# The opening of layer 0: banks and signals of their own for the first two batches, VectorE normalising them, and three small loads moved to SyncE

## What is computed

```
x = x + L0_xattn(layernorm(x), ctx, ctx)      # 16 heads of 8 features, softmax, biases bq, bk, bv, bo
x = x + L0_ffn(layernorm(x))                  # 8 experts, chosen per position by affinity to waff
x = x + L1_xattn(layernorm(x), ctx)           # 16 heads of 64 features, its own layernorms, one null key
x = x + L1_ffn(layernorm(x))                  # gate, up and down with rounded weights and activations

def L0_xattn(q, k, v):                        # per batch
    q, k, v = q @ Wq.T + bq, k @ Wk.T + bk, v @ Wv.T + bv
    attn = softmax(q_h @ k_h.T / sqrt(8))     # per head h
    return concat(attn @ v_h) @ Wo.T + bo
```

## Time and profile before

| | us |
|---|---|
| median of three runs | 879.06 |
| lowest and highest | 878.26 and 881.53 |
| the profiled execution, its own time | 880.04 |
| its span in the profile | 878.3 |
| PE busy | 810.5 (92%) |
| DVE busy | 698.3 (80%) |
| POOL busy | 482.5 (55%) |
| ACT busy | 443.5 (50%) |

### The profile page before, as it was taken

How to read it: one execution, slowest core, us unless ns; L and a number is a source line. 1 busy time by engine, 2 the same in 40 slices (tenths; PEclk the granted TensorE clock), 3 DMA queues, 4 the chain that set the end, 5 groups by cost and what they waited for, 6 DMA issues and landing times. The chain is left out here.

```text
span 878.3 us, 29798 instructions
## 1 busy us (share of the span) xinstructions
PE 810.5 (92%) x11109; PEld 674.8 (77%) x11139; DVE 698.3 (80%) x1919; ACT 443.5 (50%) x1077; POOL 482.5 (55%) x975
## 2 busy tenths in 40 slices
PE   4999999997499997899999999999999999999983
PEld 2777777775498886778888888888888888888861
DVE  3889989875514555478999999899999999999876
ACT  2666666654055564344555545455455554555442
POOL 7567678875512224244655656466564655656243
PEclk9999999998789997799999999999999999999995
DMA  9766330000655662021211212112121121211110
GB/s 242 273 247 247 119 104 14 15 20 26 166 149 142 162 159 69 10 60 35 56 45 35 69 36 60 45 36 69 35 64 41 47 57 35 66 39 48 42 32 12
DMA packets 57666, 70.91 MB, mean 81 GB/s; under 512 B 8002, under 2 KB 34482, under 8 KB 57522
## 3 DMA queue, kind: packets, MB, share of 16 engines
q1 hardware_dynamic: 42226, 44.55, 19.9%
q10 hardware_dynamic: 13248, 20.26, 6.3%
q0 software_dynamic: 2048, 4.20, 1.6%
HBM read 44.61 MB, written 24.37 MB: 79 GB/s over the span
## 5 line engine op out<-in xcount | busy, mean ns | idle before, releaser
L1943 ACT ACTIVATE a_pT<-psum 128x512 f32<-128x512 f32 x128 | 69.5, 595 | 40.8 <-PE psum L1745 22.2
L664 DVE TENSOR_REDUCE l_mx<-psum 128x4 bf16<-128x512 f32 x128 | 81.8, 680 | 7.4 <-remote 4.4
L2107 DVE TENSOR_REDUCE a_mxf<-psum 128x4 f32<-128x512 f32 x128 | 81.0, 673 | 3.1 <-PE psum L1718 3.1
L1473 POOL TENSOR_TENSOR f_hd<-f_hmc,f_wmean 128x1 f32<-128x1 f32 x32 | 6.7, 211 | 135.0 <-DVE f_hr L2224 134.2
L1650 PEld LDWEIGHTS psum<-a_cTm,a_Wk 128*128 128x128 f32 x512 | 67.8, 199 | 15.7 <-issue 14.4
L499 ACT ACTIVATE l_pT<-psum 128x512 f32<-128x512 f32 x128 | 71.2, 598 | 14.4 <-PE psum L385 13.8
L1638 PEld LDWEIGHTS psum<-a_xT,a_Wq 128*128 128x128 f32 x512 | 66.1, 196 | 15.3 <-issue 14.4
L1700 PE MATMUL psum<-a_Wv,a_cTm 128*128 128x512 f32 x128 | 73.7, 658 | 0.8 <-DVE a_kT L2095 0.6
L1726 PE MATMUL psum<-a_qT,a_kT 64*128 64x128 f32 x1024 | 71.8, 281 | 0.0
L1638 PE MATMUL psum<-a_xT,a_Wq 128*128 128x128 f32 x512 | 71.1, 283 | 0.5 <-ACT a_xT L1926 0.5
L1467 POOL TENSOR_SCALAR f_hq<-f_ht 128x512 bf16<-128x512 f32 x31 | 60.3, 1945 | 20.0 <-ACT f_ht L1988 19.9
(11 more groups left out here) (308 smaller groups left out, 2244.3 us busy)
## 6 DMA issues: line engine op xcount, KB each, us to landing
sorted_x<-r_zeros ACTq DMA_DIRECT2D x12, 1408.0 KB, 5.9
a_r_all<-a_r_rows SPq DMA_DIRECT2D x62, 256.0 KB
e_w<-in_E_W1b SPq DMA_DIRECT2D x39, 258.0 KB, 2.8
e_xt<-sorted_x SPq DMA_DIRECT2D x39, 64.0 KB, 2.4
sorted_y<-e_yt ACTq DMA_DIRECT2D x39, 64.0 KB, 2.7
a_cin<-in_ctx SPq DMA_DIRECT2D x32, 64.0 KB
out<-f_x SPq DMA_DIRECT2D x32, 64.0 KB
x_res<-in_x SPq DMA_DIRECT2D x1, 512.0 KB, 7.2
```

The lines of the kernel that those rows point to most:

```text
L664: nc.vector.tensor_reduce(mx[:, s, Q4 * k:Q4 * k + Q4], maxp[k % 2].rearrange("p (h t) -> p h t", h=Q4), AX_X, ALU.max).then_inc(mx_ready, 1)
L1943: nc.scalar.activation(pT[:, 2 * half + e, :], tp[e], ACT.Exp, scale=SCALE).then_inc(exp_ready, 1)
L2107: nc.vector.tensor_reduce(mxf[:, hh:hh + 4], maxp[e].rearrange("p (h t) -> p h t", h=Q4), AX_X, ALU.max).then_inc(mxf_ready, 1)
```

## The change

Five edits, all in `attention_routing_block`.

1. **Banks and signals.** For the batches 0 and 1, k, q and v go to six different banks: k to `tp[0]` and `tp[2]`, q to `tp[1]` and `tp[3]`, v to `yp` and `xp`; the transposed x of batch 1 goes to `tp[2]`. Each of the six matmuls signals for itself, and each copy waits for its own alone. `q_spread` of these batches no longer waits for `k_copy`, and `x_transpose(1)` no longer for `v_copy(0)`. New waits: `max_scores(0, 0)` for k and q of batch 0, `scores(0)` for k and q of batch 1, `expert_sums` for `v_copy(0)`.
2. **Normalisation.** POOL makes only `l_rs` for the two batches, and DVE makes `l_xn` (a `tensor_scalar` of its own). POOL waits until both are made before its second memset of ones. `x_norm(2)` on POOL moves ahead of the small constants.
3. **Signals of the loads.** bv leaves `w_in`, of which now five loads are awaited; it counts on `v_in` together with both memsets of ones, and only `v_copy` of 0 and 1 wait for that.
4. **Loads.** waffT, bo and wo are issued by SP, after its eighth load (batches 4 to 7), no longer by ACT.
5. **Order.** PE does `x_transpose(1)`, `max_scores(0, 0)` and then `projections(1)`. DVE goes: statistics and normalisation of 0, the same of 1, `q_spread(0)`, `v_copy(0)`, `x_stats(2)`, two `maxima`, `q_spread(1)`, two `maxima`, `v_copy(1)`, `x_stats(3)`.

```diff
@@ -122,7 +122,7 @@
-    ones_set = sem("l0_ones_set")
+    v_in = sem("l0_v_in")
@@ -141,7 +141,14 @@
-    N_W, N_O = 6 * 16, 3 * 16
+    first_k, first_q, first_v = (tp[0], tp[2]), (tp[1], tp[3]), (yp, xp)
+    N_W, N_O, N_V = 5 * 16, 3 * 16, 16 + 2
...
+    def projected(b, part):
+        return 3 * b + part if b < 2 else b + 5
...
+    def first_x(b):
+        return tp[2][:, 0:S] if b == 1 else xp[:, 0:S]
@@ -157,6 +164,8 @@
+            if i == 3:
+                late_loads(sp)
@@ -165,10 +174,12 @@
-        act.dma_start(bv_row[:], w["bv"].partition_broadcast(P)).then_inc(w_in, 16)
-        act.dma_start(rt["waffT"][:], wr["waffT"]).then_inc(rsem["w_in"], 16)
-        act.dma_start(bo_row[:], w["bo"].partition_broadcast(P)).then_inc(rsem["w_in"], 16)
-        act.dma_start(wo[:], w["Wo"]).then_inc(rsem["w_in"], 16)
+        act.dma_start(bv_row[:], w["bv"].partition_broadcast(P)).then_inc(v_in, 16)
...
+    def late_loads(sp):
+        sp.dma_start(rt["waffT"][:], wr["waffT"]).then_inc(rsem["w_in"], 16)
+        sp.dma_start(bo_row[:], w["bo"].partition_broadcast(P)).then_inc(rsem["w_in"], 16)
+        sp.dma_start(wo[:], w["Wo"]).then_inc(rsem["w_in"], 16)
@@ -183,12 +194,15 @@
     def pool_part(g, after_setup, before_loop):
...
-        def x_norm(b, s):
+        def x_rsqrt(b, s):
...
+        def x_norm(b, s):
+            x_rsqrt(b, s)
@@ -257,14 +271,15 @@
-        x_norm(0, 0)
-        nc.gpsimd.memset(v[:, 0, :, HD:], 1.0).then_inc(ones_set, 1)
-        x_norm(1, 1)
-        nc.gpsimd.memset(v[:, 1:4, :, HD:], 1.0).then_inc(ones_set, 1)
+        x_rsqrt(0, 0)
+        nc.gpsimd.memset(v[:, 0, :, HD:], 1.0).then_inc(v_in, 1)
+        x_rsqrt(1, 1)
+        g.wait_ge(xn_ready, 2)
+        nc.gpsimd.memset(v[:, 1:4, :, HD:], 1.0).then_inc(v_in, 1)
...
+        x_norm(2, 0)
...
-        x_norm(2, 0)
@@ -297,10 +312,10 @@
         def x_transpose(b, s):
...
-            if b < 6:
-                wait(pe, v_ready, b)
+            if 2 <= b < 6:
+                pe.wait_ge(v_ready, b)
...
-            nc.tensor.transpose(xp[:, 0:S], xn[:, s, :], ident[:]).then_inc(xt_done, 1)
+            nc.tensor.transpose(first_x(b), xn[:, s, :], ident[:]).then_inc(xt_done, 1)
@@ -319,12 +334,18 @@
-            nc.tensor.matmul(xp[:, S:2 * S], wk[:], cT[:, b, :], start=True, stop=True)
-            nc.tensor.matmul(xp[:, 2 * S:3 * S], wq[:], xT[:, s, :], start=True, stop=True)
-            nc.tensor.matmul(xp[:, 3 * S:4 * S], cT[:, b, :], wv[:], start=True, stop=True).then_inc(qkv_done, 1)
+            kp, qp, vp = (first_k[b], first_q[b], first_v[b]) if b < 2 else (xp, xp, xp)
+            k = nc.tensor.matmul(kp[:, S:2 * S], wk[:], cT[:, b, :], start=True, stop=True)
+            if b < 2:
+                k.then_inc(qkv_done, 1)
+            q = nc.tensor.matmul(qp[:, 2 * S:3 * S], wq[:], xT[:, s, :], start=True, stop=True)
+            if b < 2:
+                q.then_inc(qkv_done, 1)
+            nc.tensor.matmul(vp[:, 3 * S:4 * S], cT[:, b, :], wv[:], start=True, stop=True).then_inc(qkv_done, 1)
...
         def expert_sums():
...
+            pe.wait_ge(v_ready, 1)
@@ -361,7 +382,10 @@
         def max_scores(b, u):
-            if u == 0 and b < 5:
+            if u == 0 and b == 0:
+                pe.wait_ge(kT_ready, 1)
+                pe.wait_ge(qz_ready, 1)
+            elif u == 0 and b < 5:
@@ -373,6 +397,9 @@
         def scores(b):
+            if b == 0:
+                pe.wait_ge(kT_ready, 2)
+                pe.wait_ge(qz_ready, 2)
@@ -413,10 +440,11 @@
-        for b in range(2):
-            x_transpose(b, b)
-            projections(b, b)
+        x_transpose(0, 0)
+        projections(0, 0)
+        x_transpose(1, 1)
         max_scores(0, 0)
+        projections(1, 1)
         max_scores(0, 1)
@@ -478,8 +506,9 @@
         def x_copy(b, s):
...
-            wait(act, qkv_done, b - 1)
-            nc.scalar.copy(xT[:, s, :], xp[:, 0:S]).then_inc(xT_ready, 1)
+            if b >= 2:
+                act.wait_ge(qkv_done, projected(b - 2, 3))
+            nc.scalar.copy(xT[:, s, :], first_x(b)).then_inc(xT_ready, 1)
@@ -489,9 +518,9 @@
         def k_copy(b, s):
...
                 act.wait_ge(w_in, N_W)
-            act.wait_ge(qkv_done, b + 1)
+            act.wait_ge(qkv_done, projected(b, 1))
...
-            nc.scalar.activation(kT[:, b % 3, :], xp[:, S:2 * S], ACT.Identity, bias=bk[:], scale=1.0).then_inc(kT_ready, 1)
+            nc.scalar.activation(kT[:, b % 3, :], (first_k[b] if b < 2 else xp)[:, S:2 * S], ACT.Identity, bias=bk[:], scale=1.0).then_inc(kT_ready, 1)
@@ -510,9 +539,10 @@
-        for b in range(2):
-            x_copy(b, b)
-            k_copy(b, b)
+        x_copy(0, 0)
+        k_copy(0, 0)
+        x_copy(1, 1)
+        k_copy(1, 1)
@@ -549,22 +579,29 @@
+        def x_norm(b, s):
+            dve.wait_ge(rs_done, 2 * b + 2)
+            nc.vector.tensor_scalar(xn[:, s, :], x_res[:, b, :], mv[:, s, 0:1], rs[:, s, 1:2],
+                                    ALU.subtract, ALU.mult).then_inc(xn_ready, 1)
...
         def q_spread(b, s):
...
-            dve.wait_ge(qkv_done, b + 1)
-            dve.wait_ge(kT_ready, b + 1)
+            dve.wait_ge(qkv_done, projected(b, 2))
+            if b >= 2:
+                dve.wait_ge(kT_ready, b + 1)
...
-                out=qz[:, b % 3, :, :], in0=xp[:, 2 * S:3 * S].unsqueeze(1).broadcast_to([P, Q4, S]), scalar=bq[:],
+                out=qz[:, b % 3, :, :], in0=(first_q[b] if b < 2 else xp)[:, 2 * S:3 * S].unsqueeze(1).broadcast_to([P, Q4, S]), scalar=bq[:],
...
         def v_copy(b, s):
...
-                dve.wait_ge(ones_set, b + 1)
+                dve.wait_ge(v_in, N_V)
+                dve.wait_ge(qkv_done, projected(b, 3))
...
-            nc.vector.tensor_tensor(v[:, b % 4, :, 0:HD], xp[:, 3 * S:4 * S].rearrange("p (h d) -> p h d", h=H),
+            nc.vector.tensor_tensor(v[:, b % 4, :, 0:HD], (first_v[b] if b < 2 else xp)[:, 3 * S:4 * S].rearrange("p (h d) -> p h d", h=H),
@@ -690,15 +727,20 @@
-        for b in range(2):
-            x_stats(b, b)
-        for b in range(2):
-            q_spread(b, b)
-            v_copy(b, b)
-        for b in range(2, 4):
-            x_stats(b, b % 2)
-        for k in range(4):
-            maxima(0, 0, k)
+        x_stats(0, 0)
+        x_norm(0, 0)
+        x_stats(1, 1)
+        x_norm(1, 1)
+        q_spread(0, 0)
+        v_copy(0, 0)
+        x_stats(2, 0)
+        maxima(0, 0, 0)
+        maxima(0, 0, 1)
+        q_spread(1, 1)
+        maxima(0, 0, 2)
+        maxima(0, 0, 3)
+        v_copy(1, 1)
+        x_stats(3, 1)
```

## The result

The changed kernel takes 867.29 us in the median of four runs (866.05 to 875.41), the kernel before 878.8 (878.26 to 881.53): the ratio is 0.9888, with a 95% interval of 0.9851 to 0.9925. It is faster, as forecast, but by 11.5 us in the medians where 6.3 was said, and the median lies outside the range of 870.8 to 875.4.

What follows compares the result with a forecast made beforehand. The opening was taken as a chain of waits, with PE nearly full after it. An earlier scores(0), 5.6 us, plus 0.7 for TensorE's clock gave 6.3 us, for a median of 872.8 us, range 870.8 to 875.4.

Steps and rivals of the forecast that it cites:

- The chain of the opening: From batch 0's normalisation to the exact scores: scores(0) starts at 11.55 instead of 17.18, a gain of 5.6 us.
- GpSimd's shift: x_plus(0) on POOL starts at about 17 instead of 20.60, a shift of 3.6 us, with nobody waiting.
- the three loads: waffT, bo and wo, issued by SP, land behind batches 4 to 7; nothing is charged for them.
- Their rivals: Loop start: POOL sets the pace, 875.5 us (7 in 100); the three loads come late, about 875 (6 in 100).
- the blocked clears: ACT's early clears block ScalarE, up to 7.1 us each: 879.9 for one, 887 for two; 4 in 100.
- The clock: TensorE can be at the high level when scores(0) starts: 0.7 us gained, between 0 and 1.6.
- the bounds: Total gain: 5.45 us with long normalisation and no clock gain, 7.45 with the short one and all of it.
- Then each stage of the rest as long as before: Sign for all stages after the opening: they keep their lengths, so nothing is charged there.
- The range: Whole kernel's median: 870.8 to 875.4 us, from the sum's bounds, the scatter of a median and the rivals at 875.
- the 6.3 of the sum: Whole kernel: 5.6 us from the opening's chain plus 0.7 from TensorE's clock.

Runs made afterwards that it cites:

- e14: The changed kernel unaltered, on a later chip: 868.68 us, ratio 0.9921 to the kernel before.
- e8: The changed kernel with six extra matmuls on TensorE ahead of x_transpose(0): 869.84 us, against 870.18 for the changed kernel.
- e5: The changed kernel unaltered, run again beside the kernel before on another chip: 870.18 against 876.96 us, ratio 0.9906.
- e15: The changed kernel with six extra matmuls ahead of x_transpose(0), run once more on a later chip: 871.7 us.
- e7: The kernel before with the edit of the loads alone (bv not awaited by PE, three loads issued by SyncE): 877.34 against 876.96 us, ratio 0.999.
- e13_matched: The changed kernel with eight reciprocals on VectorE before q_spread(1), scores(0) at 17.65: 875.39 against 876.81 us before, ratio 0.9992.
- e6: The kernel before unaltered, one execution with its profile: scores(0) at 17.72 us.
- the three delays: The changed kernel with one, two or five reciprocals on VectorE before q_spread(1): 862.98, 864.52 and 866.89 us, against 870.53 for the kernel before.
- e4_before_late2: The kernel before with two reciprocals ahead of its first maxima: 872.19 us, against 870.53 without them.
- e1 to e4: Late starts by reciprocals on VectorE: the changed kernel with five, one and two (866.89, 862.98, 864.52 us), the kernel before with two (872.19).
- e9 to e12: The changed kernel with GpSimd normalisation, without GpSimd's wait, with the old order (scores(0) at 11.60, 11.47, 12.73 us), or with 46 extra matmuls (861.52 us).

## Why the prediction was right and wrong

- **The chain of the opening** was right link by link, and its sum, 5.6 us, was 6.05 in the first pair of traces. The small excess of 0.4: the memset and the normalisation overlap less badly than charged (5.20 against 5.44), the second memset ended at 8.1 and not 8.6, so that `v_copy(0)` did not wait, and the copies passed on sooner. Against a second trace of before, with bv 0.54 later, it is 6.6.
- **GpSimd's shift** of 3.9 us (20.60 to 16.74) with nobody waiting, and **the three loads** hidden: right. Their rivals, and that of the blocked clears, fell: ACT ran its squares of waffT right behind its second copy of k, at 10.06, and no clear was blocked though each went out 5 us earlier.
- **The clock** was the step of the mechanism that failed: "so it can be at the high level when `scores(0)` starts: 1.1 us more", taken at 0.7 "between 0 and 1.6". In none of the three traces of the changed kernel was it: `scores(0)` took 2.09, 2.09 and 1.81 us (e14), against 1.14 at the high level in e8. In the first trace the clock came up at 17.6 us, and the loop's lead shrank from 6.05 to 5.0, so the term was -1.05 there. In e5 and e14 it came up before 14.5 and 13. The work before it does not fix its time: the same instructions at the same times got it 3 to 5 us apart, in e8 and e15 over 9 us apart (5.3 against after 14). In all traces but that of e8 it came after `scores(0)` had begun, by 1.5 us (e14) to some 9 (e7). The Trainium skill (TensorE: Matmul & The Clock Gate, "Part 1: The HAM clock gate") says that the gate's watch runs freely and that the same kernel meets it at a different point in each run; the traces agree that the moment differs, the reason they do not show. Over the traces with a plain opening the loop was entered at 16.1 to 18.2 after and at 23.2 and 25.1 before, so the lead is 5.0 to 9.0 us where the bounds were 5.45 to 7.45.
- **"Then each stage of the rest as long as before"** is the step that put the result outside the range: the sum charged nothing for all that follows, and in the first pair of traces that nothing was 7.0 us. e13_matched shows that at most some 3 us of it can belong to the edits (the lower end of its interval). The rest is scatter, or hangs on the time at which the stages begin, and much of it is the clock: the granted clock from 40 to 370 us was 0.92 in the first trace of before and 0.94 in that of the changed kernel, but 0.94 in e6, which has none of the edits, and 0.91 in e13, which has all. The 11.5 us of four executions against four (10.3 in the means) are 2 to 3.5 more than the 8 of the larger samples, and that was luck; the four themselves lie from 866.05 to 875.41.
- **The range** was too narrow because "the scatter of a median" was read off three runs 3.3 us apart and counted as about 1 us. The kernel before spreads over 10 us in 25 runs, and its standard deviation was 1.8 to 2.9 us on the four later chips, so medians of three and four runs differ by chance by some 2 us.
- **What stays open**: the gains on the two larger samples, 8.0 and 7.9 us in the means, and the three delays given back, 7.4 to 8.6, are all above the 6.3 of the sum. A lead of 5.0 to 9.0 at the loop's entry, by the clock, could cover them, but too few traces exist to say that its mean is 8 and not 6.5. On the chip of the delays it does not: against e4_before_late2, with its 1.6 us taken off, `q_spread(3)` is 5.1, 4.4 and 1.7 us ahead for one, two and five reciprocals, where the mean gains are 7.8, 6.0 and 3.4. And layer 1, from its first to its last `a_oT`, took 475.3, 477.2, 475.8 and 473.2 us in the four traces of the kernel before and its variants (before, e6, e7, e4), but 471.2 to 474.7, in the mean 473.3, in the 13 traces with all or most edits; 472.1 in e13. The granted clock was 1.00 in all. That would be 2 us for theory B, from an effect that nobody has named; with four traces it can be chance, and the mean time of e13 does not show it.

## What to carry to other kernels

Where a stage is a chain of short waits ahead of a long full one, price the change at the one event that opens the full stage, link by link; that came out within half a microsecond here. But a term that hangs on TensorE's clock, and every comparison of single executions beyond that event, needs the scatter of this kernel over many runs, not of three. To ask whether an edit does more than move the start, put the start back with a delay and keep the edit, and run it often enough: a dozen executions against 28 tell 2 us here, not 1.

## What the runs showed that was not expected

- GpSimd's memsets blocked VectorE's normalisation from SBUF to SBUF (0.34 us alone, 1.67 beside them), and a second memset on end kept it blocked. A wait that orders the memset behind it costs nothing here and saves 0.34 us at `scores(0)` (11.47 against 11.13).
- The kernel before took 870.53, 876.96, 869.45 and 876.81 us on four chips, and 878.8 at the start. From `q_spread(25)`, at some 155 us, to the first tile of the experts the traces of e1 to e4 and e9 to e12 took 72.4 to 74.7 us and all others 80.0 to 84.5, in both kernels alike, so times of different occasions are not to be compared.
- The windows report a granted clock of 1.00 through the opening, while the lengths of equal matmuls halve within it (1.06 to 0.61 us for eight of `minus_max`): in that stretch the durations tell the level and the column does not.
